# Decays of two steps in one ScalarE instruction, products of four steps in one GpSimd instruction

## The reference

```
dA = exp(dt_t[:, :, None] * A)          # the decay
dB = dtN_t * B_t
h  = dA * h + dB[:, None, :] * x_t[:, :, None]
y  = einsum('bdn,bn->bd', h, C_t) + Dskip * x_t
```

## Time and profile before

| what | value |
|---|---|
| median of three executions | 3903.39 us |
| profiled execution, its span | 3906.9 us |
| PE busy | 3163.4 us (81%) |
| DVE busy | 2983.4 us (76%) |
| POOL busy | 2909.4 us (74%) |
| ACT busy | 2553.7 us (65%) |
| last product starts at | 3422.6 us |

### The profile page before, as it was taken

How to read it: one execution, slowest core, us unless ns; L and a number is a source line. 1 busy time by engine, 2 the same in 40 slices (tenths; PEclk the granted TensorE clock), 3 DMA queues, 4 the chain that set the end, 5 groups by cost and what they waited for, 6 DMA issues and landing times.

```text
span 3906.9 us, 68984 instructions
## 1 busy us (share of the span) xinstructions
PE 3163.4 (81%) x17390; PEld 2012.8 (52%) x17390; DVE 2983.4 (76%) x5234; ACT 2553.7 (65%) x6158; POOL 2909.4 (74%) x3055
## 2 busy tenths in 40 slices
PE   5687888778889888988889887988889888776772
PEld 3233354335556555655556555655556555566662
DVE  3698989988898888878897788888898788822110
ACT  3455677457867777676867777676867777665451
POOL 1465757686769886888868897888968887966755
PEclk9788999789989998999989999999989999988896
DMA  3965656465869677886869677886869677856773
GB/s 89 221 146 129 157 124 162 120 161 137 221 177 263 153 211 197 222 221 163 233 178 244 158 208 194 231 212 162 231 185 260 157 202 195 235 150 182 241 233 109
DMA packets 420323, 730.02 MB, mean 187 GB/s; under 512 B 56203, under 2 KB 313814, under 8 KB 417750
## 3 DMA queue, kind: packets, MB, share of 16 engines
q1 hardware_dynamic: 302422, 484.13, 49.7%
q10 hardware_dynamic: 99072, 203.47, 17.0%
q0 software_dynamic: 18432, 37.93, 3.5%
HBM read 596.93 MB, written 100.07 MB: 178 GB/s over the span
## 4 chain that ended last, share of the span: by engine, by line
PE 24%; POOL 22%; issue 21%; DVE 15%; ACT 11%; DMA 4%; ACTq 2%; SPq 1%; POOLq 1%; DVEq 0%; PEldq 0%
POOL prod L698 10%; DVE state L1582 6%; PE ps_conv L901 5%; PE ps_main L967 4%; DVE ps_x L1569 3%; POOL got L821 3%; PE ps_g L1085 2%; DMA dt_rep<-dt_dram 2%; POOL rows_in L798 2%; PE ps_g L1092 2%; POOL hidden L810 2%; PE ps_y L981 2%; ACT dt_rep L1206 2%; PE ps_h L1073 2%; PE ps_x L915 1%
## 5 line engine op out<-in xcount | busy, mean ns | idle before, releaser
L698 POOL TENSOR_TENSOR prod<-state,c_rep 128x384 f32<-128x384 f32 x1536 | 1532.7, 1007 | 608.5 <-DVE state L1582 588.7
L1582 DVE TENSOR_TENSOR_SCAN state<-dt_rep,carry,ps_x 128x384 f32<-128x384 f32 x1280 | 1285.8, 1005 | 0.0
L1569 DVE TENSOR_TENSOR ps_x<-ps_x,db_rep 128x384 f32<-128x384 f32 x1536 | 852.9, 555 | 243.0 <-PE ps_x L915 223.7
L1206 ACT ACTIVATE dt_rep<-dt_rep,vecs 128x384 f32<-128x384 f32 x1536 | 917.8, 615 | 137.9 <-DMA dt_rep<-dt_dram 77.7
L915 PE MATMUL ps_x<-x_stack,copy 96*128 96x384 bf16 x1536 | 534.2, 350 | 310.8 <-DVE state L1582 306.4
L901 PE MATMUL ps_conv<-gx,w_conv 128*128 128x384 f32 x1728 | 689.6, 507 | 8.0 <-DVE parts L1599 4.6
L915 PEld LDWEIGHTS ps_x<-x_stack,copy 96*128 96x128 bf16 x1536 | 153.9, 100 | 681.6 <-DVE state L1582 493.1
L1390 ACT ACTIVATE g_sb<-ps_g,w_down 128x128 f32<-128x128 f32 x1032 | 304.2, 371 | 231.1 <-PE ps_g L1092 226.3
L901 PEld LDWEIGHTS ps_conv<-gx,w_conv 128*128 128x128 f32 x1728 | 301.1, 195 | 216.6 <-issue 129.6
L1073 PE MATMUL ps_h<-u_t,w_up 128*128 128x128 f32 x2064 | 327.5, 298 | 104.0 <-DVE silu L1799 80.0
L810 POOL TENSOR_TENSOR hidden<-g_sb,silu 128x384 f32<-128x384 f32 x344 | 343.7, 999 | 83.9 <-ACT u_out L1396 74.8
(11 more groups left out here) (256 smaller groups left out, 4958.7 us busy)
## 6 DMA issues: line engine op xcount, KB each, us to landing
dt_rep<-dt_dram SPq DMA_DIRECT2D x384, 768.0 KB
w_up<-in_w_exp ACTq DMA_DIRECT2D x344, 384.0 KB
w_down<-in_w_exp ACTq DMA_DIRECT2D x344, 193.5 KB
x_stack<-parts SPq DMA_DIRECT2D x576, 48.0 KB
u_in<-rows_in SPq DMA_DIRECT2D x344, 64.5 KB
rows_out<-u_out SPq DMA_DIRECT2D x344, 64.0 KB
dt_dram<-dt SPq DMA_DIRECT2D x192, 96.0 KB
qv<-in_x SPq DMA_DIRECT2D x48, 192.0 KB
```

Of the source, the lines that this page charges most:

```text
L698: pool.tensor_tensor(prod[:, k % HS, :], state[:, k % HS, :], c_rep[:, c % 2, :], ALU.mult).then_inc(s_prod.sem, 1)
L1206: act.activation(dt_rep[:, g % XS, q, :], dt_rep[:, g % XS, q, :], ACT.Exp, scale=decay_rate).then_inc(s_decay.sem, 1)
L1569: dve.tensor_tensor(x_n, x_n, db_rep[:, c % 2, :], ALU.mult).then_inc(s_inflow.sem, 1)
L1582: dve.tensor_tensor_scan(state[:, k % HS, :], dt_rep[:, g % XS, q, :], ps_x[k % XB][:, 0:T], init, ALU.mult, ALU.add).then_inc(s_state.sem, 1)
```

## The change

`decay` returns at odd steps, and at even ones does two steps in one activation of 768 elements per partition, adding 2 to the semaphore `s_decay`. It is called with k + 3, so at odd k it now does the decays of k + 3 and k + 4. `product` returns unless its step is the last of a quad, and then multiplies the four states of the quad, 1536 elements per partition, with the chunk's C, read four times by a broadcast over the quad. It waits for the scan of the last step of the quad, and adds 4 to `s_prod`.

```diff
             def product(i, k):
-                if i is None:
+                if i is None or k % QD != QD - 1:
                     return
                 c, n = divmod(k, NB)
-                if n == 0:
+                s = (k - 3) % HS
+                if n == QD - 1:
                     pool.wait_ge(*read(i, f"C{c}"))
                 due(pool, s_state, i, k + 1)
                 due(pool, s_fold, i, (k - HS) // QD + 1)
-                pool.tensor_tensor(prod[:, k % HS, :], state[:, k % HS, :], c_rep[:, c % 2, :], ALU.mult).then_inc(s_prod.sem, 1)
+                pool.tensor_tensor(prod[:, s:s + QD, :], state[:, s:s + QD, :],
+                                   c_rep[:, c % 2, :].unsqueeze(1).broadcast_to([P, QD, T]), ALU.mult).then_inc(s_prod.sem, QD)
...
                 i, k = (w.i, k) if k < SC else (w.nx, k - SC)
                 if i is None:
                     return
+                if k % 2:
+                    return
                 g, q = divmod(k, QD)
                 if q == 0:
                     due(act, s_rep[g % XS], i, g // XS + 1)
-                act.activation(dt_rep[:, g % XS, q, :], dt_rep[:, g % XS, q, :], ACT.Exp, scale=decay_rate).then_inc(s_decay.sem, 1)
+                act.activation(dt_rep[:, g % XS, q:q + 2, :], dt_rep[:, g % XS, q:q + 2, :], ACT.Exp, scale=decay_rate).then_inc(s_decay.sem, 2)
```

## The result

The changed kernel takes 3928.8 us (median of 6 runs, 3919.45 to 3931.38), the kernel before 3906.28 on the same chip (6 runs, 3900.72 to 3915.9): ratio 1.0053 with a 95% interval of 1.0041 to 1.0065 (the quotient of the two medians, 1.0058, lies inside it). It is slower by half a per cent. 3917 was forecast, inside a range of 3868 to 3958. The profiled execution has a span of 3927.6 us, 20.7 more than before.

What follows compares the result with a forecast made beforehand. It saw no single bound, but three nearly equal engines (TensorE, VectorE, GpSimd) handing over small pieces. Terms -13 - 27 + 10 + 4 + 40 = +14 on the 3906.9 us span, less 3.5, gave 3917 us, range 3868 to 3958.

Steps and rivals of the forecast that it cites:

- the port: VectorE instructions with SBUF operands wait until GpSimd's instruction in progress ends, longer behind quads in routing steps; +40 us.
- the marks it set: Profile signs of being right: instruction times, routing-line medians, VectorE busy 30 to 60 us more, TensorE's product waits under 100.
- Decays, forecast -13: On ScalarE, a pair of decays in one activation saves 0.17 us; by their 2% of the chain, -13 us.
- four steps expected to pay about 1.5 us together: Routing steps 132, 136, 140 and 144, where VectorE's instructions meet the last third of a quad; about +1.5 us together.
- Products, forecast -27: On GpSimd, a quad saves 0.44 us, 169 us in all; from the products' 10% of the chain, -27 us taken.
- fold with gate, forecast +14: TensorE's folds wait for later quads, +10 us; GpSimd's rectify and gate behind the waiting quad come 2.4 us later, +4.
- the fold's cover: Time between a quad's last scan and TensorE's fold: fold 0.45 us late in fast stretch, hidden by 1.2 in full stretch.
- Rival A: The relief of GpSimd and ScalarE wins over port and fold; 3868 us, chance 0.27.
- Rival B: All cancels: port +24, fold and gate +10, gains -34; 3903 us, chance 0.26.
- Rival C: Quads make TensorE late: 128 folds at 0.6 us, +77 on top of the port, less gains; 3980 us, chance 0.07.

Runs made afterwards that it cites:

- e4: The kernel before with quads of products only in the 24 routing steps (124 to 147), single products elsewhere and single decays; ratio 1.0073 to the kernel before.
- e1: The kernel before with only the decays in pairs, products still single; ratio 0.9955 to the kernel before.
- e10: The changed kernel with nearly all quads cut to 96 of 384 positions per step, leaving out three quarters of the products; ratio 0.9757 to the kernel before.
- e9: The changed kernel with each quad issued as four single products of 384 elements, all after the fourth scan; ratio 1.0135 to the kernel before.
- e8: The changed kernel with products of three steps plus one single outside the routing steps, all single inside; ratio 0.9986 to the kernel before.

## Why the prediction was right, and where its terms were off

**Direction and mechanism.** The forecast was slower, by the port, and that stands: e4 shows it by itself, in the steps named, as VectorE's busy time. Most of the marks it set came true: quads of 3449 ns, decays of 934 ns, L1711 at 3274 ns, L1703 and L1708 back at their least (308 and 174 ns at the median), the waits of TensorE's weight loads for products at 59.4 us, between 28.7 and 100. Two did not: L1726 has a median of 518 ns where 3 us or more were named, and VectorE's +24.5 us lies under the 30 to 60. The time is 12 us above the 3917, the ratio +0.53% where +14 us are +0.36%. Behind that stands a sum whose large terms were off on both sides, so that the nearness of the number is in part luck.

**Decays, forecast -13.** e1 measures -17.6 us by the ratio and -10.5 between the profiled spans. A pair holds ScalarE for 904.71 - 903.88 = 0.83 us in e1, where 0.85 was taken:

```profile
903.88 0.94 ACT L1208 ACTIVATE dt_rep<-dt_rep,vecs 128x768 f32<-128x768 f32 x1
904.71 0.49 ACT L1320 ACTIVATE ps_main<-ps_main 128x384 f32<-128x384 f32 x1
```

A pair so saves 0.19 and not 0.17. The Trainium skill (ScalarE: Activation LUTs, "What ACT_TABLE_LOAD costs"), set aside in the prediction for the bound of the rows, gave 0.19; the trace agrees.

**The port, forecast +40 (48 us of VectorE).** In size it failed: the nine lines rose by 22.0 us in the changed kernel, VectorE as a whole by 24.5. L1691 and L1711 rose by 10.6 and 15.3 us where 15 and 18 were expected; L1691 was held for its full 3.3 to 3.4 us in four images of seven only. The step that failed is L1726: +18 expected, -5.8 measured. It was to start behind the quad of step 143 and starts ahead of it:

```profile
2027.47 0.52 DVE L1730 TENSOR_TENSOR big_k<-iota,tally 128x344 f32<-128x344 f32 x1
```
```profile
2027.58 3.70 POOL L699 TENSOR_TENSOR prod<-state,c_rep 128x1536 f32<-128x1536 f32 x1 [3.48 <-DVE state L1586]
```

It came first by 0.11 us, and the quad takes 3.70 us in place of 3.44. In the kernel before, the product had come first by only 0.03 us:

```profile
2004.41 0.99 POOL L698 TENSOR_TENSOR prod<-state,c_rep 128x384 f32<-128x384 f32 x1 [0.27 <-DVE state L1582]
```
```profile
2004.44 1.33 DVE L1726 TENSOR_TENSOR big_k<-iota,tally 128x344 f32<-128x344 f32 x1
```

By the traces, a single product that waited for its scan started 0.08 us after the scan's end (median of 518), a pair 0.13 and a quad 0.13 or 0.22 (median of 140: 0.22). The short quads of e10 start as late as the long ones, so this goes with the form of the instruction, not with its length. A tenth of a microsecond in who comes first is worth 2.6 us. The margin of 0.03 us could be read before the change; the later start of a joined instruction could not. L1677, one of four steps expected to pay about 1.5 us together in an image, went from 647 to 2271 ns by itself (+11.6 us in all), and L1714 paid 6.0 us that the prediction didn't count.

**Products, forecast -27, and fold with gate, forecast +14.** Together -13 was expected of these. Measured is VectorE's idle time of the changed kernel over that of e1: +8.4 us. No run separates the two terms, since whatever shortens GpSimd's work also moves the end of its products. What the runs show: products bunched 2.4 us later than in e1, at 24 us less work of GpSimd, cost 74.0 us of idle time (e9), and a bunch that is 0.4 us shorter gives 66 of it back (the changed kernel). At the 0.05 us per us that e10 measured, the relief of 190 us would be about -9, and at most -13 by e10's time (78 us for 1126); that is an estimate, and a third to a half of the forecast's -27. The step at fault is that the term was taken from the products' share of the chain. What is left, +17 to +22, would be the lateness, where +14 was forecast. The two rows from which the fold's cover was read are the tight end: in the kernel before, a fold starts 6.65 us after its quad's last scan in the mean, against the 3.1 and 5.3 of the earlier trace rows.

**The sum.** For the quads alone the prediction had -27 + 10 + 4 + 40 = +27. The profiled spans of the changed kernel and e1 differ by 31.2, of which 23.7 are VectorE busy and 8.4 idle; by the ratios it is 0.98%, 38 us. So it was near by errors that cancel: the port 16 us too high and the rest 21 too low, both by the profiled executions. Rival A (3868) fell with GpSimd's relief. Rival B (3903, all of it cancels) fell too, for the interval of the ratio leaves out 1. Rival C (3980) was right in kind, for the weight loads waited for products at 65 places where there were 47, but not in size. The upper end of the range is a slip: the middle between the forecast and C is 3949, not 3958. The measured 3928.8 lies inside either.

**What stays open.** Why the costs of quads inside and outside the routing steps don't add up, beyond the 7.4 us of L1691; the 0.31% between e8 and e1; how much of the idle time goes with the granted clock; and how the 8.4 us of idle time that the quads add over e1 split between folds, statistics on GpSimd (`st` waits for `qv`, 33.2 us against 17.3 in e1) and the queue behind the waiting quad (`hidden` waits for `silu`, 60.3 us against 3.4). A fold one step later was not tried, nor a kernel whose last product is early while GpSimd has fewer instructions.

## What to carry to other kernels

Joining the instructions of one engine saves its fixed cost each time, and charges the others the whole length: they get the first piece only with the last, and instructions of another engine that contend with it stand still until the one long instruction is over, as the small VectorE instructions of the routing did here. Join where the consumer has several steps of slack and no other engine is held up (ScalarE's decays, +0.45% of speed); on GpSimd look first at which small VectorE instructions follow the same event. Split the span into the busy and idle time of the engine that leads: in these kernels the port showed as busy time at an equal count of instructions (e4), lateness as idle time (e9), and what mended the one did not mend the other.

## What the hardware showed that I had not expected

- The hold chains: three small VectorE instructions in a row each waited for another GpSimd instruction (3.32, 1.73 and 1.05 us); each time GpSimd's next instruction had started 0.11 us before VectorE's. Cutting one of them in two moved the wait from 1736 + 309 to 925 + 1058 ns.
- The eight-element scan of the routing, the old L1708, waits as well (878 ns against 174), while the large scans with one operand in PSUM take 1.00 us beside a quad: at 2028.58, 1.00 us into the quad of 2027.58, one lasts 1.00.

```profile
2028.58 1.00 DVE L1586 TENSOR_TENSOR_SCAN state<-dt_rep,carry,ps_x 128x384 f32<-128x384 f32 x1
```

- A joined product starts later after the scan that it waits for, 0.13 or 0.22 us in place of 0.08, and that alone decided which engine held up the other in step 143.
- The same move of the folds, 0.6 us later in both, cost 0.65% with single products and 1.2% with quads.
